# Two tail units of a bilinear interaction kernel moved within the hand-written order

## The chip, the core and the metric

The kernel runs on one core of a Trainium2 chip. The metric is device time in microseconds (us) of one launch, from the first to the last instruction and what lies around them. Inputs and outputs lie in the chip's memory (HBM); the host only rearranges them.

## What is computed

For each of 512 samples, 200 feature vectors of 64 numbers are multiplied by a 64x64 matrix of their own field, and each result is scored against all 200 feature vectors of the sample. All is float32.

```python
def _L0_rec_ref(feature, weight):        # feature (512, 200, 64), weight (200, 64, 64)
    bilinear = jnp.einsum('bie,ied->bid', feature, weight)
    out = jnp.einsum('bid,bjd->bij', bilinear, feature)
    return out                           # (512, 200, 200), 82 MB
```

## The kernel before

The samples are worked through in 4 groups of 128. In a group, the 200 fields of the first factor are taken in 3 chunks of 64 fields, and a tail of 8 fields (192 to 199). There are four kinds of units of TensorE work, and each writes one pair of PSUM banks (a unit number n uses the pair n mod 4):

- a **mix** unit (L263 to L288) multiplies 16 fields by their weights, 64 matmul rows in the profile (two for each float32 matmul in the program). Four mix units make the `mixed` operand of one chunk. ScalarE and VectorE copy each into `mixed` (L367 to L378).
- a **score** unit (L311 to L326), 16 matmul rows, scores four samples of a chunk. Two of them make an output tile: its first half is copied from PSUM to SBUF by ScalarE, its second by VectorE (L357 to L360). A chunk has 8 output tiles. Tile 1.4 is here the tile with t = 4 (the fifth) of chunk 1.
- a **tail_mix** unit (L298 to L309) does the 8 fields of the tail, once in a group, and the copies go into `tails`.
- two **tail** units per group (L328 to L344), 64 matmul rows each, score the tail fields of all samples of the group. They make one output tile together, the first unit's half copied by ScalarE and the second's by VectorE (L362 to L365).

A function `walk` (L74 to L96) is the order of all units, written by hand. TensorE, ScalarE and VectorE all run it, so a unit stands at the same place in each queue. While chunk c is scored, the mix units of the next chunk are put in behind tiles 1, 3, 5 and 6, and tail_mix behind tile 6 of chunk 0. `TAIL_CHUNK` and `TAIL_AFTER` (L42, L43) say behind which tiles the two tail units stand.

An output tile is 0.8 MB. It is written to one of 6 slots in SBUF, and the slot is the number of the tile mod 6. A tile gets its number (the list OUT_TILES, L114 and L119) when its *second* unit comes in the order. The copy of either half waits until the tile with the number six lower has been stored from that slot and has landed (L353, L354). SyncE issues the stores in the order of the numbers, when both halves are copied (L190 to L200), two issues of 400 KB each. Behind the stores of the tiles of chunk 0 it issues the next group's first loads, and behind those of chunk 2 (L206 to L210) the next group's second loads. In chunk 1 there are no loads. Group 3 has no next group, and no loads. A unit of TensorE waits for the copies of the unit four before it, which had the same banks (`wait_bank`, L233 to L240).

Of the kernel before, what the change touches and what calls it, by code (L numbers as in the profile page):

```python
# [6 lines left out]
GROUPS = 4  # L7
# [5 lines left out]
CHUNK, CHUNKS = 64, 3  # L13
# [25 lines left out]
LAST_WAITED = MIX_AFTER[(PART - CHUNK) // MIX_FIELDS]  # L39


TAIL_CHUNK = [1] * (GROUPS - 1) + [CHUNKS - 1]  # L42
TAIL_AFTER = [(2, 4)] * (GROUPS - 1) + [(5, 7)]  # L43
SLOTS = 6

WARM_UPS = 8
# [23 lines left out]
def next_chunk(g, c):  # L70
    return (g, c + 1) if c + 1 < CHUNKS else (g + 1, 0)


def walk(score, tail, mix, tail_mix):  # L74


    n = 0
    for m in range(MIX_UNITS):
        mix(n, 0, 0, m)
        n += 1  # L80
    for g in range(GROUPS):
        for c in range(CHUNKS):
            for t in range(TILES):
                for u in range(2):
                    score(n, g, c, t, u)
                    n += 1
                if c == TAIL_CHUNK[g] and t in TAIL_AFTER[g]:
                    tail(n, g, TAIL_AFTER[g].index(t))
                    n += 1
                to, chunk = next_chunk(g, c)  # L90
                if t in MIX_AFTER and to < GROUPS:
                    mix(n, to, chunk, MIX_AFTER.index(t))
                    n += 1
                if c == 0 and t == TAIL_MIX_AFTER:
                    tail_mix(n, g)
                    n += 1  # L96


def count_copies():

    copies, readers, number, tiles = [], [], {}, []

    def add(n, act, dve, banks, *key):
        a, d = copies[-1] if copies else (0, 0)
        copies.append((a + act, d + dve))
        readers.append(banks)
        number[key] = n

    def score(n, g, c, t, u):
        add(n, u == 0, u == 1, ((u,), (u,)), "score", g, c, t, u)
        if u == 1:
            tiles.append(("score", g, c, t))  # L114

    def tail(n, g, e):
        add(n, e == 0, e == 1, ((e,), (e,)), "tail", g, e)
        if e == 1:
            tiles.append(("tail", g))  # L119

    def mix(n, g, c, m):
        add(n, 1 if m % 2 == 0 else 2, 2 if m % 2 == 0 else 1, ((m % 2,), (1 - m % 2,)), "mix", g, c, m)

    def tail_mix(n, g):
        add(n, 1, 1, ((0, 1), ()), "tail_mix", g)

    walk(score, tail, mix, tail_mix)
    return copies, readers, number, tiles
# [6 lines left out]
def build(nc, x, weight, out, out_tail):  # L135
# [36 lines left out]
    with nc.Block() as block:  # L172
# [59 lines left out]
        def _(pe):  # L232
# [112 lines left out]

            warm_up()
            walk(score, tail, mix, tail_mix)

        def copies(eng, copy, engine):
# [37 lines left out]
            for n in range(MIX_UNITS):  # L387
                own = slice(n * OWN_FIELDS, (n + 1) * OWN_FIELDS)
                eng.wait_ge(w_loaded[n], 16)
                copy(w_sb[half_rows(engine), 1, own, :], w_sb[half_rows(1 - engine), 0, own, :]).then_inc(  # L390
                    w_crossed[engine], 1)
            walk(score, tail, mix, tail_mix)

        @block.scalar
# [42 lines left out]
```

## Time and profile before

| | |
|---|---|
| median of three runs | 311.1 us (307.51 to 311.19) |
| the profiled execution | 306.8 us, of which the span of instructions is 305.0 us |
| TensorE matmul busy | 243.2 us, 80% |
| VectorE busy | 152.8 us, 50% |
| ScalarE busy | 130.1 us, 43% |
| GpSimd busy | 12.5 us, 4% |
| DMA | 112.35 MB, mean 368 GB/s; the main queue's packets take 92.6% of 16 engines' span |
| mean granted TensorE clock | 0.961 of full speed |

In the profile PE is TensorE, PEld its weight loads, ACT ScalarE, DVE VectorE, POOL GpSimd and SP SyncE; "q" behind a name is its sequencer, which issues DMA. A row of the page that groups instructions has the line of the kernel, the engine, the operation, out<-in, and the count.

### The profile page before, as it was taken

How to read it: one execution, taken by the hardware profiler on the slowest of the kernel's cores; microseconds unless marked ns; L12 is line 12 of the kernel's file. 1: busy time of each engine (PE TensorE's matmuls, PEld its weight loads, DVE VectorE, ACT ScalarE, POOL GpSimd, SP SyncE). 2: the span in 40 equal slices, each digit the busy share in tenths (PEclk: the TensorE clock that was granted, in tenths of full speed). 3: DMA queues.
4: the chain of work that ended last, by engine and by line, in shares of the span. 5: the costliest groups of instructions: out<-in, count | busy, mean ns of one | idle time of the engine just before them, and what ended most of it. 6: DMA issues, size and time to landing. Idle time of an engine off the chain costs nothing.

```text
span 305.0 us, 14640 instructions
## 1 busy us (share of the span) xinstructions
PE 243.2 (80%) x6800; PEld 210.9 (69%) x6800; DVE 152.8 (50%) x180; ACT 130.1 (43%) x181; POOL 12.5 (4%) x23
## 2 busy tenths in 40 slices
PE   6839849999877586999867785898985774998990
PEld 2437749888776476878866675866885674996970
DVE  0153634556755443537644454634765554775621
ACT  2153515445544324245444243542653451665420
POOL 2004800000000000000000000000000000000000
PEclk9996997999999979899999799999999999999997
DMA  7999997999999999968999999986999999599995
GB/s 219 415 417 357 363 410 302 324 376 373 369 360 416 407 419 420 409 280 354 374 366 408 383 411 417 388 355 248 389 371 391 408 387 417 210 402 381 409 408 218
DMA packets 22172, 112.35 MB, mean 368 GB/s; under 512 B 4320, under 2 KB 4320, under 8 KB 21856
## 3 DMA queue, kind: packets, MB, share of 16 engines
q1 hardware_dynamic: 22112, 111.43, 92.6%
q8 instruction: 53, 0.87, 1.1%
q14 instruction: 7, 0.06, 0.0%
HBM read 29.49 MB, written 81.92 MB: 365 GB/s over the span
## 4 chain that ended last, share of the span: by engine, by line
PE 76%; issue 16%; DMA 2%; SPq 2%; DVE 1%; ACT 1%
PE psum L322 50%; PE psum L285 17%; PE psum L339 8%; DMA w_sb<-w_dram 2%; SPq L166 2%; PE psum L305 1%; DVE tile L355 1%; ACT mixed L376 0%; ACT w_sb L390 0%; SPq L178 0%
## 5 line engine op out<-in xcount | busy, mean ns | idle before, releaser
L322 PE MATMUL psum<-x_sb,mixed 64*64 64x200 f32 x3072 | 163.1, 351 | 14.0 <-issue 12.5
L322 PEld LDWEIGHTS psum<-x_sb,mixed 64*64 64x64 f32 x3072 | 133.3, 139 | 27.9 <-issue 17.9
L355 DVE COPY tile<-psum 128x800 f32<-128x800 f32 x100 | 99.2, 992 | 88.6 <-PE psum L322 79.8
L355 ACT COPY tile<-psum 128x800 f32<-128x800 f32 x100 | 82.4, 826 | 70.2 <-PE psum L322 54.0
L285 PE MATMUL psum<-x_sb,w_sb 64*64 64x64 f32 x3072 | 64.4, 221 | 35.1 <-issue 34.2
L285 PEld LDWEIGHTS psum<-x_sb,w_sb 64*64 64x64 f32 x3072 | 61.7, 134 | 40.5 <-issue 37.7
L376 ACT COPY mixed<-psum 64x512 f32<-64x512 f32 x48 | 27.8, 580 | 43.2 <-PE psum L285 42.6
L376 DVE COPY mixed<-psum 64x512 f32<-64x512 f32 x48 | 33.1, 689 | 16.7 <-PE psum L285 15.5
L378 ACT COPY mixed<-psum 128x512 f32<-128x512 f32 x24 | 14.1, 586 | 36.3 <-PE psum L285 36.2
L378 DVE COPY mixed<-psum 128x512 f32<-128x512 f32 x24 | 16.6, 691 | 22.3 <-PE psum L285 22.2
L339 PE MATMUL psum<-x_sb,tails 128*32 128x200 f32 x512 | 25.0, 342 | 0.1
L339 PEld LDWEIGHTS psum<-x_sb,tails 128*32 128x32 f32 x512 | 16.9, 108 | 7.5 <-issue 2.5
L296 PE MATMUL psum<-tails 128*128 128x512 f32 x16 | 9.9, 790 | 2.6 <-POOL tails L216 2.6
L227 POOL COPY w_sb<-w_sb 64x512 f32<-64x512 f32 (+1 forms) x18 | 10.5, 586 | 25.7 <-DMA w_sb<-w_dram 24.1
L296 PEld LDWEIGHTS psum<-tails 128*128 128x128 f32 x16 | 4.0, 260 | 7.6 <-issue 5.0
L390 DVE COPY w_sb<-w_sb 64x512 f32<-64x512 f32 x4 | 1.7, 422 | 13.9 <-DMA w_sb<-w_dram 13.9
L305 PE MATMUL psum<-x_sb,w_sb 64*64 64x64 f32 x128 | 5.6, 240 | 2.2 <-issue 2.2
L390 ACT COPY w_sb<-w_sb 64x512 f32<-64x512 f32 x4 | 2.5, 617 | 11.3 <-DMA w_sb<-w_dram 11.2
L305 PEld LDWEIGHTS psum<-x_sb,w_sb 64*64 64x64 f32 x128 | 5.1, 155 | 2.3 <-issue 2.3
L385 DVE COPY tails<-psum 64x512 f32<-64x512 f32 x4 | 2.8, 694 | 3.9 <-PE psum L305 3.9
L385 ACT COPY tails<-psum 64x512 f32<-64x512 f32 x4 | 2.3, 580 | 2.6 <-PE psum L305 2.6
L216 POOL MEMSET tails<- 128x2048 f32 x1 | 1.8, 1804 | 0.3 <-POOLq L418 0.3
(5 smaller groups left out, 1.7 us busy)
## 6 DMA issues: line engine op xcount, KB each, us to landing
out_dram<-tile SPq DMA_DIRECT2D x192, 400.0 KB, 5.6
x_sb<-x_dram SPq DMA_DIRECT2D x64, 400.0 KB, 6.9
out_tail_dram<-tile SPq DMA_DIRECT2D x8, 400.0 KB, 4.2
w_sb<-w_dram SPq DMA_DIRECT2D x1, 1152.0 KB, 15.2
w_sb<-w_dram SPq DMA_DIRECT2D x4, 256.0 KB, 7.3
w_sb<-w_dram SPq DMA_DIRECT2D x1, 1024.0 KB, 13.1
```

Source lines behind the costliest of these rows:

```text
L166: eng.dma_start(x_sb[strip, 2 * (g % 2), quads], x[g, 0, strip, quads]).then_inc(part0_loaded[g % 2], 16)
L227: nc.gpsimd.tensor_copy(w_sb[half_rows(h), 1, own, :], w_sb[half_rows(1 - h), 0, own, :]).then_inc(w_crossed[2], 1)
L285: last = nc.tensor.matmul(psum[half_rows(h ^ swap), bank + swap, r * HALF_SAMPLES:(r + 1) * HALF_SAMPLES], w_field(h, field), x_field(g, h ...
L296: nc.tensor.matmul(psum[:, 2 * BANK_PAIRS - 1, :], zeros[:, 0:128], zeros, start=True, stop=True)
L305: last = nc.tensor.matmul(psum[half_rows(h), n % BANK_PAIRS * 2, r * HALF_SAMPLES:(r + 1) * HALF_SAMPLES], w_field(h, TAIL_FIRST + r), x_f ...
L322: last = nc.tensor.matmul(psum[half_rows(pair), n % BANK_PAIRS * 2 + h, a * FIELDS:(a + 1) * FIELDS], mixed[half_rows(h), (CHUNKS * g + c) ...
L339: last = nc.tensor.matmul(psum[column * TAIL_TILE:(column + 1) * TAIL_TILE, n % BANK_PAIRS * 2 + half_unit, piece * FIELDS:(piece + 1) * F ...
L355: copy(tile[:, k % SLOTS, engine], psum[:, bank:bank + 2, 0:2 * FIELDS]).then_inc(copied[engine], 1)
L376: copy(to[half_rows(h)], source[half_rows(1 - h)]).then_inc(copied[engine], 1)
L378: copy(to, source).then_inc(copied[engine], 1)
L385: copy(tails[half_rows(engine), :, 0:4:3, engine, :], source).then_inc(copied[engine], 1)
L390: copy(w_sb[half_rows(engine), 1, own, :], w_sb[half_rows(1 - engine), 0, own, :]).then_inc(w_crossed[engine], 1)
```

## The change

For the groups 0 to 2, the first tail unit stands behind tile 4 of chunk 1 instead of tile 2, and the second behind tile 1 of chunk 2 instead of tile 4 of chunk 1. For that, the table names a chunk with each tile. Group 3 is as before: behind tiles 5 and 7 of chunk 2. Lines behind the table are one line higher up in the changed kernel (L355 is L354, L339 is L338).

```diff
-TAIL_CHUNK = [1] * (GROUPS - 1) + [CHUNKS - 1]
-TAIL_AFTER = [(2, 4)] * (GROUPS - 1) + [(5, 7)]
+TAIL_AFTER = [((1, 4), (2, 1))] * (GROUPS - 1) + [((2, 5), (2, 7))]
...
-                if c == TAIL_CHUNK[g] and t in TAIL_AFTER[g]:
-                    tail(n, g, TAIL_AFTER[g].index(t))
+                if (c, t) in TAIL_AFTER[g]:
+                    tail(n, g, TAIL_AFTER[g].index((c, t)))
```

On TensorE, from tail_mix of group 0 (L305) on, before; L322 is score (16 matmuls of the program for a tile), L285 mix, L339 a tail unit:

```order
L305 MATMUL psum<-x_sb,w_sb 64x64 x16
L322 MATMUL psum<-x_sb,mixed 64x200 x48
L285 MATMUL psum<-x_sb,w_sb 64x64 x32
L322 MATMUL psum<-x_sb,mixed 64x200 x16
L339 MATMUL psum<-x_sb,tails 32x200 x32
L322 MATMUL psum<-x_sb,mixed 64x200 x16
L285 MATMUL psum<-x_sb,w_sb 64x64 x32
L322 MATMUL psum<-x_sb,mixed 64x200 x16
L339 MATMUL psum<-x_sb,tails 32x200 x32
L322 MATMUL psum<-x_sb,mixed 64x200 x16
L285 MATMUL psum<-x_sb,w_sb 64x64 x32
L322 MATMUL psum<-x_sb,mixed 64x200 x16
```

The same place in the changed kernel:

```order
L304 MATMUL psum<-x_sb,w_sb 64x64 x16
L321 MATMUL psum<-x_sb,mixed 64x200 x48
L284 MATMUL psum<-x_sb,w_sb 64x64 x32
L321 MATMUL psum<-x_sb,mixed 64x200 x32
L284 MATMUL psum<-x_sb,w_sb 64x64 x32
L321 MATMUL psum<-x_sb,mixed 64x200 x16
L338 MATMUL psum<-x_sb,tails 32x200 x32
L321 MATMUL psum<-x_sb,mixed 64x200 x16
L284 MATMUL psum<-x_sb,w_sb 64x64 x32
L321 MATMUL psum<-x_sb,mixed 64x200 x16
L284 MATMUL psum<-x_sb,w_sb 64x64 x32
L321 MATMUL psum<-x_sb,mixed 64x200 x48
```

The first tail unit has moved behind two more tiles and a mix unit, to where the second was; the second has left the chunk and follows the last row shown (tile 7 of chunk 1 and tiles 0 and 1 of chunk 2 are the x48).

On ScalarE, from tile 1.2 of group 0 on, before. L355 is the copy of a tile's half, and slot_out is the semaphore of the slot that it writes; the second row is the first tail unit's:

```order
L355 COPY tile<-psum 128x800 [waits slot_out4,unit_ready]
L355 COPY tile<-psum 128x800 [waits slot_out1,unit_ready]
L355 COPY tile<-psum 128x800 [waits slot_out5,unit_ready]
L376 COPY mixed<-psum 64x32x16 [waits unit_ready]
L376 COPY mixed<-psum 64x32x16
L355 COPY tile<-psum 128x800 [waits slot_out0,unit_ready]
L355 COPY tile<-psum 128x800 [waits slot_out2,unit_ready]
```

The same place in the changed kernel, with the first tail unit's copy the second of the two that one row counts (x2):

```order
L354 COPY tile<-psum 128x800 [waits slot_out4,unit_ready]
L354 COPY tile<-psum 128x800 [waits slot_out5,unit_ready]
L375 COPY mixed<-psum 64x32x16 [waits unit_ready]
L375 COPY mixed<-psum 64x32x16
L354 COPY tile<-psum 128x800 [waits slot_out0,unit_ready] x2
L354 COPY tile<-psum 128x800 [waits slot_out1,unit_ready]
```

The tail's copy stood between the slots 4 and 5 and wrote slot 1; it now stands directly behind the copy of tile 1.4 and writes the slot of that tile, slot 0.

## Rows read from the trace of the kernel before

**Rows 1.** The page: the chain of work that ended last, by engine.

```profile
PE 76%; issue 16%; DMA 2%; SPq 2%; DVE 1%; ACT 1%
```

**Rows 2.** Busy sums by chunk, from chunk 2 of group 0 on; columns in the header.

```profile
core 0: us, PE busy (x) PEld busy (x) DVE busy (x) ACT busy (x) POOL busy (x), PEclk, DMA share, GB/s
...
72.00:91.50 19.50, 16.94 (x516) 15.20 (x512) 12.06 (x14) 10.10 (x15) 0.00 (x0) 1.00 0.98 367
91.50:120.00 28.50, 19.45 (x550) 17.27 (x547) 13.72 (x16) 11.37 (x16) 0.00 (x0) 0.94 1.02 415
120.00:143.65 23.65, 23.52 (x641) 19.46 (x640) 11.94 (x14) 10.14 (x15) 0.00 (x0) 0.93 0.87 351
143.65:165.60 21.95, 16.52 (x518) 15.48 (x514) 12.00 (x14) 10.89 (x15) 0.00 (x0) 1.00 0.99 380
165.60:191.30 25.70, 18.95 (x548) 18.25 (x549) 12.69 (x15) 10.25 (x15) 0.00 (x0) 0.93 1.02 406
191.30:216.50 25.20, 22.84 (x650) 18.20 (x642) 12.93 (x15) 10.59 (x16) 0.00 (x0) 1.00 0.84 334
216.50:236.65 20.15, 15.99 (x516) 14.91 (x513) 12.07 (x14) 10.07 (x15) 0.00 (x0) 1.00 1.00 384
```

**Rows 3.** Timeline of TensorE, chunk 1 of groups 1, 2, 0: start, us, what.

```profile
127.32 3.11 PE L339 MATMUL psum<-x_sb,tails 128*32 128x200 f32 x64
130.37 1.66 PE L322 MATMUL psum<-x_sb,mixed 64*64 64x200 f32 x32
...
139.78 1.60 PE L322 MATMUL psum<-x_sb,mixed 64*64 64x200 f32 x32
...
206.66 0.58 PE L322 MATMUL psum<-x_sb,mixed 64*64 64x200 f32 x7 [1.29 <-issue]
...
212.61 0.71 PE L322 MATMUL psum<-x_sb,mixed 64*64 64x200 f32 x12
...
67.80 0.52 PE L322 MATMUL psum<-x_sb,mixed 64*64 64x200 f32 x6
```

**Rows 4.** Timeline of SyncE, issues of stores: start, us, what.

```profile
58.92 0.94 SPq L200 DMA_DIRECT2D out_dram<-tile  x1
63.58 1.11 SPq L200 DMA_DIRECT2D out_dram<-tile  x2
66.58 1.85 SPq L200 DMA_DIRECT2D out_tail_dram<-tile  x2
135.56 1.11 SPq L200 DMA_DIRECT2D out_dram<-tile  x2
138.57 1.11 SPq L200 DMA_DIRECT2D out_tail_dram<-tile  x2
208.37 1.11 SPq L200 DMA_DIRECT2D out_dram<-tile  x2
211.40 1.11 SPq L200 DMA_DIRECT2D out_tail_dram<-tile  x2
```

**Rows 5.** DMA issues at 136.08, 208.88, 286.04, each alone; last column us to landing.

```profile
out_dram<-tile SPq DMA_DIRECT2D x1, 400.0 KB, 4.4
...
out_dram<-tile SPq DMA_DIRECT2D x1, 400.0 KB, 3.1
...
out_dram<-tile SPq DMA_DIRECT2D x1, 400.0 KB, 6.0
```

**Rows 6.** Busy sums around the places where stores run dry, columns as in rows 2.

```profile
57.00:66.00 9.00, 9.00 (x240) 7.04 (x233) 3.16 (x4) 3.64 (x5) 0.00 (x0) 1.00 1.01 415
...
131.50:134.00 2.50, 2.50 (x104) 2.23 (x100) 1.64 (x2) 1.64 (x3) 0.00 (x0) 1.00 0.30 114
...
139.50:147.00 7.50, 7.50 (x255) 6.64 (x251) 5.72 (x8) 5.05 (x7) 0.00 (x0) 1.00 0.95 380
...
190.00:204.00 14.00, 12.93 (x360) 10.95 (x356) 6.79 (x8) 6.12 (x8) 0.00 (x0) 1.00 1.01 399
```

**Rows 7.** Timeline of ScalarE: the first tail unit's copy in group 3 and two more.

```profile
292.13 2.29 ACT L355 COPY tile<-psum 128x800 f32<-128x800 f32 x3 [3.89 <-DMA out_dram<-tile]
```

## The prediction, made before the changed kernel ran

> **What bounds the kernel now.** I read the page first. The chain that ended last is 76% TensorE work and 16% "issue", pauses that no semaphore of the program explains, and almost no copy or transfer [rows 1]. That would say: TensorE is the bound, so move work into its pauses. I then cut the span at the first scoring matmul of each chunk and read the busy sums per stage [rows 2]. It shows two regimes. In chunks 0 and 2 of the groups 0 to 2 the 16 DMA engines are saturated (share 0.98 to 1.02), while TensorE stands still for 2.6 us (72.0 to 91.5), 9.05 us (91.5 to 120.0), 5.4 us (143.65 to 165.6) and 6.8 us (165.6 to 191.3). These stages also carry the loads of the next group. Chunk 1 has no loads and both tail units: there TensorE is busy nearly throughout (23.52 of 23.65 us in group 1, 22.84 of 25.20 in group 2) and the DMA engines are at 0.87 and 0.84, that is 3.1 and 4.0 us of nothing to move. So the group from 91.5 to 165.6, 74.1 us, is some 71 us of saturated DMA time and 3 us in which the stores ran dry. A DMA gap is made up for nowhere, as far as the stages on both sides stay at a share of 1; a TensorE gap is, in the pauses of chunks 0 and 2. I therefore price the change by what it does to the moments at which the DMA engines run dry and start again, and keep the TensorE view as a rival.
>
> **What the tail units cost where they stand.** One is 3.05 us of TensorE (127.32 to the next unit's start at 130.37) [rows 3]. Its copy is 0.83 us on ScalarE (in group 3: 2.29 for that one and two more in a row, 0.76 to 0.83 each; I take 0.83) [rows 7], and each store of a tile takes two issues on SyncE.
>
> **The change.** No instruction is added or removed; two are moved, in three groups.
>
> *Second unit, to chunk 2.* 3.05 us of TensorE and 0.8 MB of store leave chunk 1 and come in between tiles 1 and 2 of chunk 2. DMA time is conserved. TensorE there idles 2.6, 5.4 and (216.5 to 236.65) 4.2 us [rows 2], so the unit can go under DMA time already spent; cost 0 in the DMA view. If that cover is gone it is 3.05 us per group, 9.2 in all. The next group's second load is one issue that follows on SyncE behind tile 1 of chunk 2 and ahead of the tail's store, so it isn't delayed. VectorE's copy there finds its slot free, since ScalarE has waited for the same slot in chunk 1.
>
> *First unit, behind tile 4 of chunk 1.* This is the one with a price. Output tiles are numbered when they are complete, and slot = number mod 6. Before, tiles 1.0 to 1.4 completed ahead of the tail, so the first unit's copy behind tile 1.2 wrote the slot of tile 0.7, stored three tiles earlier. Now five tiles complete between the first unit and the second: 1.5, 1.6, 1.7, 2.0, 2.1. The tail's number is that of tile 1.4 plus 6, the order on ScalarE shows it (two copies in a row wait for slot_out0). So ScalarE's copy must wait for the landing of a store whose second half VectorE has not even copied yet. Queued behind it on ScalarE: its half of tile 1.5, without which SyncE cannot store 1.5, nor anything behind it. TensorE goes on for tail unit, tile 1.5 and mix unit 2 (four banks' depth), then its first unit of tile 1.6 waits for the tail's copy.
>
> How long from the first issue of a store to its landing? The trace has it at three loads. Lightly loaded, group 2: issue 208.37, second half issued 208.88, landed 3.1 later, together 3.6 us. After a gap that had just closed, group 1: 135.56, 136.08 plus 4.4, together 4.9 us. Saturated, in group 3, whose first tail unit waits in the same way, but for a tile with three more behind it (2.2, with 2.3 to 2.5 between): the second half issued at 286.04 plus 6.0, and the first 0.9 us earlier (as long as the saturated issue at 58.92 took, 0.94), together 6.9 us; ScalarE stood 3.89 us for it until 292.13 [rows 4, 5, 7]. That row proves the mechanism; the new place has no tile in between at all.
>
> Then, from landing L: tail copy 0.83 and the copy of 1.5 at 0.83, with 0.05 us steps: the store of 1.5 is issued at L + 1.75, and TensorE begins tile 1.6 at L + 0.9. I compare with the tail's store before (which was the first to restart the DMA engines there) and with tile 1.6's start.
>
> Group 0. DMA share is 1.01 from 57 to 66 [rows 6]: there is a backlog, and the same bytes lie ahead of tile 1.4, so they can't be done before 66. Tile 1.4's store started at 63.58; 3.05 earlier is 60.5, but SyncE ends the issue of tile 1.2 only at 59.86 (58.92 + 0.94), and a pair of such issues takes 1.9 us and some gap, so 1.3 at 59.9, 1.4 at 61.9 [rows 4]. I take the saturated 6.9: L = 68.8, next store 70.55 against 66.58: **+4.0 us**. Tile 1.6: 69.7 against 67.80.
> Group 1. 135.56 - 3.05 = 132.5. The engines ran dry from 131.5 on (share 0.30 to 134) [rows 6], and now would be filled earlier: between 4.9 and 6.9, I take 5.9. L = 138.4, next store 140.15 against 138.57: **+1.6**. Tile 1.6: 139.3 against 139.78.
> Group 2. 208.37 - 3.05 = 205.3, less the pause of 1.29 us in tile 1.4 [rows 3], which comes once in 128 matmul rows or so and moves behind the tail unit, where the new wait hides it: 204.0. The engines were full until then (1.01 from 190 to 204). 5.9 again: L = 209.9, next store 211.65 against 211.40: **+0.25**. Tile 1.6: 210.8 against 212.61.
>
> Sum 5.85. Against it: after their restart the engines still had small gaps in 139.5 to 147 (0.05 of 7.5 us = 0.4) which the later, denser stores close; for three groups I take 0.9, a little less than three times that since group 0 has a backlog. Net **+5 us**. The profiled execution is 306.8 us (span 305.0 and 1.8 around it): 311.8. The median is 311.1 of runs from 307.51 to 311.19, so the profiled one is at the low end; 5 us on the median is **316.1 us**, 1.6% up.
>
> Bounds of this case: with the shortest row (3.6) in groups 1 and 2, L is 136.1 and 207.6, and in group 0 not before 66, where the bytes are done; the shifts are +1.2, -0.7 and -2.0, less 0.9: -2.4. With 6.9 everywhere: 4.0 + 2.6 + 1.25 = +7.9, with no credit. So 308.7 to 319.
>
> **A rule against it.** The rows make a landing 3.6 to 6.9 us from the first issue. The Trainium skill (DMA: Bandwidth & Descriptors, "Anatomy of one DMA — SWDGE (gpsimd) path") fits one transfer as 2.0 us plus bytes over 436 GB/s, which by my estimate is 3.9 us for the two halves of a tile back to back. The trace agrees only where the engines were nearly idle (3.6); at a share of 1 it is 6.9. By that rule the wait all but disappears, which is rival 3.
>
> **Rivals.**
> 1. *TensorE carries the time, the pauses take up the second unit.* For: the chain. Against: DMA share 1 where it pauses. The starts of tile 1.6 give +1.9, -0.5, -1.8: -0.4 in all, 310.7.
> 2. *TensorE carries, and the pauses of chunk 2 stay as they are.* They come about once in 128 matmul rows whatever the rows do, so 64 more make no room: -0.4 + 9.2 = +8.8, 319.9. For: they are called "issue" and have nothing to do with a semaphore. Against: they are short or absent in chunk 1, where the DMA engines have room.
> 3. *Faster: the landing is quick and TensorE carries.* With 3.6 us in groups 1 and 2 and 4.9 from 60.5 in group 0, tile 1.6 starts at 66.3, 137.0 and 208.5: -1.5, -2.8, -4.1, sum -8.4, 302.7. It decides when the wait ends before TensorE comes to tile 1.6, 3.05 us earlier than now; L must be under 63.9, 135.8 and 207.4. For: chunk 1 of group 1 is busy on TensorE for all its length. Against: the backlog at 57 to 66 and before 204.
>
> **Chances.** Forecast case 0.46, rival 1 0.20, rival 2 0.20, rival 3 0.12, others 0.02. Two per cent (about what a measurement of this kernel can tell from no change) is 6.2 us: 304.9 and 317.3. Below lies most of rival 3: 0.11. Above lie a good third of the forecast case and most of rival 2: 0.34. Within: 0.55. The range leaves out rival 3 and the far end of rival 2: 307 to 321.
>
> **What would show it.** A new row "ACT tile <- DMA out_dram", three times more, 4 to 6 us each behind tile 1.4; TensorE standing ahead of tile 1.6 some 5, 2.6 and 2.5 us (69.7, 139.3 and 210.8 less the starts that TensorE could reach, 64.75, 136.7 and 208.3); chunk 1's DMA share lower than now or the same though the chunk has one tail unit less; chunk 2 at a share of 1. Wrong if chunk 1 is 3 us shorter in all three groups with no such wait (rival 3), or if chunk 2 grows by 3 us with its DMA share under 0.95 (rival 2).

## The result and the profile after

The changed kernel takes 321.24 us (median of 4 runs, 316.86 to 323.75) against 310.57 us (307.51 to 311.19): ratio 1.032, interval 1.020 to 1.045, so some 10 us slower. Most kernels here have some executions that are slower by one to three per cent, and the ratios in this text compare only the fast ones, so a ratio can differ a little from that of two medians. (The 310.57 us is the median of the three runs known at the forecast and a fourth.) The profiled execution has 319.98 us and a span of 318.2 us, 13.2 us over the one before, at the high end of the difference.

The timeline of ScalarE in the changed kernel, every wait that the landing of a store ended (start us, us, what, in brackets the idle time ahead of it):

```profile
67.83 1.55 ACT L354 COPY tile<-psum 128x800 f32<-128x800 f32 x2 [7.32 <-DMA out_dram<-tile]
142.84 1.55 ACT L354 COPY tile<-psum 128x800 f32<-128x800 f32 x2 [7.40 <-DMA out_dram<-tile]
219.67 1.55 ACT L354 COPY tile<-psum 128x800 f32<-128x800 f32 x2 [6.48 <-DMA out_dram<-tile]
305.91 2.29 ACT L354 COPY tile<-psum 128x800 f32<-128x800 f32 x3 [4.71 <-DMA out_dram<-tile]
```

Before, only the last of them was there, in group 3 [rows 7]. Each of the three new ones is a first tail unit's copy, and the copy of tile 1.5 that had stood behind it follows at once (x2). The timeline of TensorE has what waits for it, tile 1.6 in groups 0, 1 and 2:

```profile
68.71 1.68 PE L321 MATMUL psum<-x_sb,mixed 64*64 64x200 f32 x32 [1.62 <-ACT tile L354]
...
143.72 1.92 PE L321 MATMUL psum<-x_sb,mixed 64*64 64x200 f32 x32 [2.62 <-ACT tile L354]
...
220.55 1.67 PE L321 MATMUL psum<-x_sb,mixed 64*64 64x200 f32 x32 [1.44 <-ACT tile L354]
```

Before, these starts had no idle time ahead [rows 3]. The chain of work now has transfers in it:

```profile
PE 67%; issue 15%; DMA 9%; SPq 3%; DVE 2%; ACT 2%; ACTq 0%
```

against 76% TensorE and 2% DMA [rows 1]. The issues of the stores of tile 1.4 and of the next tile in groups 0, 1, 2, from the timeline of SyncE:

```profile
61.34 1.90 SPq L199 DMA_DIRECT2D out_dram<-tile  x2
69.41 1.11 SPq L199 DMA_DIRECT2D out_dram<-tile  x2
136.39 1.12 SPq L199 DMA_DIRECT2D out_dram<-tile  x2
144.42 1.11 SPq L199 DMA_DIRECT2D out_dram<-tile  x2
213.67 1.78 SPq L199 DMA_DIRECT2D out_dram<-tile  x2
221.25 1.11 SPq L199 DMA_DIRECT2D out_dram<-tile  x2
```

From the end of the one issue to the start of the next SyncE issues nothing for 6.2, 6.9 and 5.8 us in the middle of each chunk 1; behind tile 1.4 it was 1.9 us before (66.58 less 64.69) [rows 4]. And the busy sums by chunk, with the columns of rows 2; chunks 1 and 2 of groups 0, 1 and 2:

```profile
49.55:72.65 23.10, 19.70 (x585) 16.76 (x577) 12.00 (x14) 9.93 (x16) 0.00 (x0) 1.00 0.76 295
72.65:97.10 24.45, 20.71 (x580) 18.63 (x580) 13.04 (x15) 10.88 (x15) 0.00 (x0) 0.93 0.98 376
...
121.95:149.15 27.20, 20.98 (x577) 17.73 (x580) 11.02 (x13) 10.28 (x15) 0.00 (x0) 0.94 0.79 318
149.15:173.15 24.00, 19.32 (x579) 16.68 (x573) 12.97 (x15) 10.45 (x15) 0.00 (x0) 0.98 0.94 357
...
200.95:224.50 23.55, 20.46 (x586) 17.62 (x578) 12.03 (x14) 9.86 (x15) 0.00 (x0) 0.96 0.77 295
224.50:250.00 25.50, 20.30 (x580) 18.36 (x580) 13.06 (x15) 10.87 (x15) 0.00 (x0) 0.95 1.00 384
```

Two things stand in them. Chunk 1 has a tail unit less and is still no shorter in sum (73.85 us for three; before it was 71.05, with the 22.2 us of group 0 in the row below), and its DMA share fell to 0.76 to 0.79. Chunk 2 grew in all three groups, 24.45, 24.0 and 25.5 us against 19.5, 21.95 and 20.15 [rows 2], far more in groups 0 and 2 than the 3 us of the unit that came in. The row of the kernel before for chunk 1 of group 0:

```profile
49.80:72.00 22.20, 22.16 (x646) 18.84 (x637) 13.06 (x15) 10.52 (x16) 0.00 (x0) 1.00 0.84 325
```

### The profile page after: what moved, and what is told of

It reads as the page before. It is cut to its first block, busy times and chain, and to the rows that moved or that the text cites. A ratio compares the mean times of both kernels' runs of the same rounds, so it can differ in the third digit from the quotient of the medians.

```text
span 318.2 us, 14640 instructions
## 1 busy us (share of the span) xinstructions
PE 251.6 (79%) x6800; PEld 218.6 (69%) x6800; DVE 152.9 (48%) x180; ACT 129.2 (41%) x181; POOL 12.5 (4%) x23
## 4 chain that ended last, share of the span: by engine, by line
PE 67%; issue 15%; DMA 9%; SPq 3%; DVE 2%; ACT 2%; ACTq 0%
PE psum L321 46%; PE psum L284 15%; DMA out_dram<-tile 7%; PE psum L338 4%; DMA w_sb<-w_dram 2%; SPq L165 2%; DVE tile L354 2%; ACT tile L354 1%; PE psum L304 1%; SPq L199 1%; ACT mixed L375 1%; DVE mixed L375 0%; DVE mixed L377 0%; ACT w_sb L389 0%; SPq L177 0%
## 5 line engine op out<-in xcount | busy, mean ns | idle before, releaser
L321 PE MATMUL psum<-x_sb,mixed 64*64 64x200 f32 x3072 | 169.7, 362 | 20.9 <-issue 9.9
L321 PEld LDWEIGHTS psum<-x_sb,mixed 64*64 64x64 f32 x3072 | 140.3, 144 | 34.9 <-issue 14.8
L354 DVE COPY tile<-psum 128x800 f32<-128x800 f32 x100 | 99.2, 992 | 104.8 <-PE psum L321 96.0
L354 ACT COPY tile<-psum 128x800 f32<-128x800 f32 x100 | 82.2, 827 | 78.7 <-PE psum L321 50.0
L284 PE MATMUL psum<-x_sb,w_sb 64*64 64x64 f32 x3072 | 65.7, 223 | 30.5 <-issue 29.4
L377 ACT COPY mixed<-psum 128x512 f32<-128x512 f32 x24 | 14.1, 588 | 37.4 <-PE psum L284 37.4
L338 PE MATMUL psum<-x_sb,tails 128*32 128x200 f32 x512 | 25.6, 343 | 1.8 <-issue 1.8
L338 PEld LDWEIGHTS psum<-x_sb,tails 128*32 128x32 f32 x512 | 17.5, 108 | 9.2 <-issue 4.6
L304 PE MATMUL psum<-x_sb,w_sb 64*64 64x64 f32 x128 | 5.3, 233 | 3.3 <-issue 3.3
L389 ACT COPY w_sb<-w_sb 64x512 f32<-64x512 f32 x4 | 2.5, 618 | 11.6 <-DMA w_sb<-w_dram 11.5
```

The costliest lines, as they stand in the source:

```text
L284: last = nc.tensor.matmul(psum[half_rows(h ^ swap), bank + swap, r * HALF_SAMPLES:(r + 1) * HALF_SAMPLES], w_field(h, field), x_field(g, h ...
L304: last = nc.tensor.matmul(psum[half_rows(h), n % BANK_PAIRS * 2, r * HALF_SAMPLES:(r + 1) * HALF_SAMPLES], w_field(h, TAIL_FIRST + r), x_f ...
L321: last = nc.tensor.matmul(psum[half_rows(pair), n % BANK_PAIRS * 2 + h, a * FIELDS:(a + 1) * FIELDS], mixed[half_rows(h), (CHUNKS * g + c) ...
L338: last = nc.tensor.matmul(psum[column * TAIL_TILE:(column + 1) * TAIL_TILE, n % BANK_PAIRS * 2 + half_unit, piece * FIELDS:(piece + 1) * F ...
L354: copy(tile[:, k % SLOTS, engine], psum[:, bank:bank + 2, 0:2 * FIELDS]).then_inc(copied[engine], 1)
L377: copy(to, source).then_inc(copied[engine], 1)
```

## The experiments

All ratios are to the kernel before, on the same chip, with 95% intervals.

**Is it the wait?** Three kernels. The first two choose the slot of a tile by age: at the tile's first half, take the slot whose tile has the lowest number, so the one stored longest ago.

```diff
+def place_tiles():
+    held, uses, slot_of, use_of = [-1] * SLOTS, [0] * SLOTS, {}, {}
...
+    def take(tile):
+        s = min(range(SLOTS), key=lambda s: held[s])
+        slot_of[tile], use_of[tile] = s, uses[s]
+        held[s], uses[s] = TILE_OF[tile], uses[s] + 1
...
-                if k >= SLOTS:
-                    eng.wait_ge(slot_out[k % SLOTS], STRIP_STORES * (k // SLOTS))
+                slot, before = SLOT_OF[name], USE_OF[name]
+                if before:
+                    eng.wait_ge(slot_out[slot], STRIP_STORES * before)
```

*The changed order with oldest slots.*

> The changed order of units, but each output tile takes the slot whose tile was stored longest ago at the moment of its first half, instead of number mod 6. The first tail unit behind tile 1.4 then waits for tile 0.7 (five tiles earlier) and not for tile 1.4 itself. Theory A (the slot wait costs it all, the second unit is hidden in chunk 2): the three ScalarE waits of 5 to 7 us are gone, and tile 1.5's store is issued some 1.5 us earlier than in the kernel before; 300 to 306 us, so faster than the kernel before by 2 to 3%. Theory B (the second unit is not hidden in chunk 2 and costs 3 us per group there): the same waits are gone, but the time is 308 to 314 us, no better than before.

Measured: 0.998 (0.993 to 1.003). Its trace has not one ScalarE wait for a store any more. So the loss is gone, and nothing is won: both theories were right on the wait, and the time (median 310.05 us) is the one of theory B. Its busy sums by chunk, same columns and same chunks as above:

```profile
47.70:70.40 22.70, 20.59 (x582) 17.66 (x578) 11.96 (x14) 10.41 (x15) 0.00 (x0) 0.98 0.89 354
70.40:95.35 24.95, 20.39 (x583) 18.35 (x577) 13.04 (x15) 10.61 (x15) 0.00 (x0) 0.95 0.94 360
...
120.65:143.95 23.30, 19.22 (x576) 16.51 (x575) 11.06 (x13) 10.10 (x15) 0.00 (x0) 1.00 0.92 372
143.95:166.80 22.85, 19.43 (x579) 17.12 (x577) 12.98 (x15) 10.92 (x15) 0.00 (x0) 1.00 0.97 362
...
193.05:216.05 23.00, 19.47 (x584) 16.85 (x575) 11.97 (x14) 10.59 (x16) 0.00 (x0) 1.00 0.88 358
216.05:239.65 23.60, 19.55 (x584) 16.52 (x580) 13.07 (x15) 10.14 (x15) 0.00 (x0) 1.00 0.99 380
```

In chunk 2 TensorE's idle time is 4.56, 3.42 and 4.05 us, 12.0 in sum, against 2.56, 5.43 and 4.16, 12.15, before [rows 2]: the pauses did not take the unit up, they stand beside it, and the three stages are 9.8 us longer. In chunk 1, where 9.2 us of TensorE work left, 7.2 us of idle time came in (9.7 us now, 59.3 busy of 69.0, for 2.5 before in the same three stages). Nearly all of it is "issue", pauses for which the profile shows no releaser. The DMA share there rose to about 0.9. The work left the chunk, and pauses came in where it had been.

*The order of the kernel before with oldest slots*, the control.

> The order of units of the kernel before, with the same choice of slots by oldest store: the control for the other one. Only the wait of 3.9 us in group 3 has reason to shrink (the copy then waits for tile 2.0 instead of 2.2). Both theories: 307 to 311 us, within 1% of before. If it is faster by 2% or more, the choice of slots gains something that has nothing to do with the moved units.

Measured: 0.9995 (0.993 to 1.006). The choice of slots alone is worth nothing, so the first kernel's ratio is the order's.

*The wait put back.* The changed order with oldest slots, and one wait added by hand:

```diff
+                    if e == 0 and g < GROUPS - 1:
+                        last = "score", g, 1, 4
+                        eng.wait_ge(slot_out[SLOT_OF[last]], STRIP_STORES * (USE_OF[last] + 1))
```

> The changed order with oldest slots (ratio 0.998), and one wait added by hand: ScalarE's copy of the first tail unit waits until tile 1.4's store has landed, as in the change. Units, slots of the other tiles and transfers are those of the fast variant. If the wait is the whole cause: ratio 1.025 to 1.035, as the change (1.032). If the slot assignment itself (which tile follows which in a slot) mattered, it stays at 0.995 to 1.01.

Measured: 1.040 (1.030 to 1.051), above the 1.025 to 1.035 that I had forecast, with an interval that overlaps that of the change. Every other slot, unit and transfer is as in the kernel with 0.998, so the wait is enough for the whole of the loss. The waits are a little longer than in the change, 8.68, 7.70 and 6.99 us. For two of the three the profile names "issue" and not the transfer; in group 0 the second half of tile 1.4's store, issued at 60.98, landed 6.9 us later, at 67.88, and the copy began at 67.95 (in group 2, 212.44 plus 5.9 is 218.34, and the copy began at 218.44):

```profile
67.95 1.55 ACT L373 COPY tile<-psum 128x800 f32<-128x800 f32 x2 [8.68 <-issue]
...
143.21 1.55 ACT L373 COPY tile<-psum 128x800 f32<-128x800 f32 x2 [7.70 <-DMA out_dram<-tile]
...
218.44 1.55 ACT L373 COPY tile<-psum 128x800 f32<-128x800 f32 x2 [6.99 <-issue]
```

**How much per microsecond of wait?** Slots by number mod 6 again, so that the place of the second unit sets which tile's landing the first one waits for.

*Second unit behind tile 1.7; the first waits for tile 1.2.*

```diff
-TAIL_AFTER = [((1, 4), (2, 1))] * (GROUPS - 1) + [((2, 5), (2, 7))]
+TAIL_AFTER = [((1, 4), (1, 7))] * (GROUPS - 1) + [((2, 5), (2, 7))]
```

> Slots by number mod 6 as in the changed kernel, but the second tail unit behind tile 1.7: the first unit's copy then waits for the landing of tile 1.2 (two tiles and a mix unit earlier) instead of tile 1.4. Theory A: landing of tile 1.2 is 5 to 6 us earlier than that of 1.4, so the ScalarE wait in chunk 1 shrinks from 5 to 7 us to 0 to 1 us and the time is that of the same order with oldest slots within 1%, 306 to 311 us. If the wait itself is not the cause, it stays at 317 to 321 us.

Measured: 1.009 (1.004 to 1.0135), within 1% of the same order with oldest slots (below), as theory A has it. But the wait did not shrink to 0 to 1 us everywhere: there are two outside group 3, of 4.99 us in group 1 and of 4.70 us in group 2.

```profile
136.70 1.55 ACT L354 COPY tile<-psum 128x800 f32<-128x800 f32 x2 [4.99 <-PE psum L321]
...
208.80 1.55 ACT L354 COPY tile<-psum 128x800 f32<-128x800 f32 x2 [4.70 <-DMA out_dram<-tile]
```

The profile puts the first down to TensorE (L321, a score unit). The tail unit that this copy reads was done at about 134.5, though (TensorE began the next unit at 134.46), and the second half of tile 1.2's store, issued at 128.96, has this row:

```profile
out_dram<-tile SPq DMA_DIRECT2D x1, 400.0 KB, 7.7
```

It landed at 136.66, and the copy began at 136.70. So this is a wait for the store too. In group 0 the copy waited only for its tail unit (2.42 us).

*The same order with oldest slots*, so without a wait.

> Oldest slot again; first tail unit behind tile 1.4 as in the change, second behind tile 1.7, so still in front of chunk 2. Against the kernel with the second behind tile 2.1 it shows what two tiles' distance is worth. Theory A: TensorE's 3 us per group are on both sides of the boundary nearly the same, but the DMA engines run dry in chunk 1 for 3 to 4 us as before: 306 to 311 us, 1 to 2% slower than with the second unit in chunk 2. Theory B: equal to it within 1%.

Measured: 1.0004 (0.9935 to 1.007), equal within the noise to the 0.998 with the second unit behind tile 2.1. That is theory B's forecast: on which side of the chunk boundary the second unit stands makes no difference that can be measured here.

*Second unit behind tile 2.0; the first waits for tile 1.3.*

```diff
+TAIL_AFTER = [((1, 4), (2, 0))] * (GROUPS - 1) + [((2, 5), (2, 7))]
```

> Slots by number mod 6, first unit behind tile 1.4, second behind tile 2.0: the first unit's copy waits for the landing of tile 1.3, which is stored one tile and a mix unit (about 2.5 us) before tile 1.4. Theory A: a ScalarE wait of about 3 to 4 us where the change has 5 to 7 us and the variant with the second unit behind 1.7 had nearly none; ratio 1.015 to 1.022, between these two (1.009 and 1.032). If the wait costs only when it is longer than some cover, it falls on one of the two.

Measured: 1.016 (1.011 to 1.021), as theory A has it, with waits of 4.35, 5.12 and 4.25 us, longer than the 3 to 4 forecast:

```profile
65.25 1.56 ACT L354 COPY tile<-psum 128x800 f32<-128x800 f32 x2 [4.35 <-DMA out_dram<-tile]
139.48 1.55 ACT L354 COPY tile<-psum 128x800 f32<-128x800 f32 x2 [5.12 <-DMA out_dram<-tile]
212.89 1.55 ACT L354 COPY tile<-psum 128x800 f32<-128x800 f32 x2 [4.25 <-DMA out_dram<-tile]
```

*The change in group 1 alone.*

```diff
+TAIL_AFTER = [((1, 2), (1, 4)), ((1, 4), (2, 1)), ((1, 2), (1, 4))] + [((2, 5), (2, 7))]
```

> The change in group 1 alone; the groups 0 and 2 keep the order of the kernel before, slots by number mod 6. Theory A (each wait costs its own DMA gap, carried to the end): a third of the loss of the whole change, ratio 1.011 to the kernel before (1.005 to 1.016), one extra ScalarE wait of 5 to 7 us. If the waits only add up when they follow each other (for instance by leaving TensorE's clock low more and more often), one alone costs under 0.5%.

Measured: 1.011 (0.9997 to 1.0225), with one such wait of 6.55 us, ahead of the copy at 142.25. The value is one third of the whole, but the interval reaches down to no loss at all, so this run alone does not decide between the two readings.

A part of such a wait costs nothing, because ScalarE would stand idle there anyway until the tail unit is computed. How long, the changed order with oldest slots shows at the same three copies, where nothing else is waited for:

```profile
63.15 1.74 ACT L373 COPY tile<-psum 128x800 f32<-128x800 f32 x2 [3.48 <-PE psum L356]
...
137.34 1.73 ACT L373 COPY tile<-psum 128x800 f32<-128x800 f32 x2 [2.90 <-PE psum L356]
...
209.91 1.72 ACT L373 COPY tile<-psum 128x800 f32<-128x800 f32 x2 [3.19 <-PE psum L356]
```

Put together, with the idle time of ScalarE ahead of these copies where a store was waited for (profiled execution, groups 0 to 2), what is left of it without the 3.48, 2.90 and 3.19 us, and the loss as (ratio - 1) of the kernel before on that chip, with its interval:

| kernel | first unit waits for | ScalarE wait, us | beyond the usual idle, us | ratio | loss, us |
|---|---|---|---|---|---|
| oldest slots | nothing late | 0 | 0 | 0.998 | -0.6 (-2.2 to 0.9) |
| second unit at 1.7 | tile 1.2 | 9.7 | 3.6 | 1.009 | 2.7 (1.3 to 4.2) |
| group 1 alone | tile 1.4 | 6.6 | 3.7 | 1.011 | 3.4 (-0.1 to 6.9) |
| second unit at 2.0 | tile 1.3 | 13.7 | 4.2 | 1.016 | 5.0 (3.5 to 6.6) |
| the change | tile 1.4 | 21.2 | 11.6 | 1.032 | 10.0 (6.1 to 13.9) |
| wait put back | tile 1.4 | 23.4 | 13.8 | 1.040 | 12.5 (9.2 to 15.7) |

Of the whole wait, 0.3 to 0.5 us of each microsecond reaches the end. Of what goes beyond the usual idle it is 0.75 to 1.2, about all of it. The intervals are wide, and each wait is that of one execution, so the second number is a fit and not a law, but one rule fits all five kernels: the first 3 us are free, and the rest is paid in full.

**What carries the time outside the wait?** The prediction rests on the DMA engines as the bound. Five kernels ask that.

*No second loads*: the loads of half of the inputs are left out for the groups 1 to 3.

```diff
-                    if c == CHUNKS - 1:
-                        for n in range(X_LOADS):
-                            if PART1_AFTER[n] == t:
-                                load_part1(sp, g + 1, n)
...
-                pe.wait_ge(part1_loaded[p], 16 * X_STRIPS * (g + 1))
+                pe.wait_ge(part1_loaded[p], 16 * X_STRIPS)
```

> The kernel before without the loads of the second half of the inputs for the groups 1 to 3 (24 issues, 9.8 MB of 112 MB; the groups use group 0's data there). TensorE's and the copies' work is unchanged. It asks what chunks 2 and 0 are bound by. If by the bytes (the DMA engines' share of 1): 9.8 MB at 415 GB/s is 23.7 us, so 285 to 292 us. If by TensorE and pauses of its own in instruction supply: 300 us or more.

Measured: 0.945 (0.9375 to 0.9525), 292.1 us. That is 16 to 17 us of 23.7, at the slow edge of the forecast for the bytes; the forecast for TensorE alone is out. TensorE's work is unchanged; what shrank is its pauses in mix and score units, from 34.2 and 12.5 us to 24.4 and 7.6. The list of waits, here (L279 is mix, L316 score; us in sum, times, longest):

```profile
PE psum L279 <- issue: 24.4, 18, 3.6
...
PE psum L316 <- issue: 7.6, 10, 1.2
```

The list of waits of the kernel before:

```profile
PE psum L285 <- issue: 34.2, 21, 3.6
...
PE psum L322 <- issue: 12.5, 8, 2.8
```

The two sums are 46.7 and 32.0 us. How far such a sum moves by itself: with all transfers left in, it is 38.2 us in the order with the second unit at 1.7 and oldest slots, whose time is that of the kernel before, and 52.3 in the kernel with three loads moved, below. So 32.0 lies outside the scatter, but how much of the 14.7 us the loads are worth is uncertain.

*No second tail unit*: two of its 32 matmuls are left in the groups 0 to 2.

```diff
-                    for piece in range(2):
-                        for pair in range(2):
-                            for column in range(4):
+                    cut = e == 1 and g < GROUPS - 1
+                    for piece in range(1 if cut else 2):
+                        for pair in range(1 if cut else 2):
+                            for column in range(1 if cut else 4):
...
-                                    x_sb[:, g % 2:g % 2 + 2, quad, :, pair], start=pair == 0, stop=pair == 1)
+                                    x_sb[:, g % 2:g % 2 + 2, quad, :, pair], start=pair == 0, stop=cut or pair == 1)
```

> The kernel before, with 2 of the 32 matmuls of the second tail unit left in the groups 0 to 2 (its output half is stored, but not computed); copies, stores and waits are unchanged. It takes 8.6 us of TensorE work out of the busy chunks 1 and no byte of output. If TensorE carries the time there (rival 2's reading: moving the unit only moves its cost): 8 to 9 us less, ratio 0.970 to 0.975. If the DMA engines carry it: the stores come 3 us earlier, run into the same transfers later, and the ratio is 0.985 to 1.0.

Measured: 0.985 (0.9735 to 0.996), 4.7 us of the 8.6. The interval reaches into both forecasts, from 1.2 to 8.2 us, so this kernel does not tell them apart; its middle is half of the work taken out. The profiled execution has TensorE busy for 243.2 us, as before, with 180 matmul rows fewer, at a mean granted clock of 0.938 instead of 0.961.

*Three of the first loads moved into the DMA gap of chunk 1.*

```diff
+PART0_AFTER = ((0, 0), (0, 1), (0, 2), (0, 3), (0, 4), (1, 3), (1, 4), (1, 5))
...
-                    if c == 0:
-                        load_part0(sp, g + 1, t)
+                    for n in range(X_LOADS):
+                        if PART0_AFTER[n] == (c, t):
+                            load_part0(sp, g + 1, n)
```

> The kernel before, with three of the eight first loads of the next group moved from behind tiles 0.5, 0.6 and 0.7 to behind tiles 1.3, 1.4 and 1.5, where the DMA engines run dry. No other edit. If the DMA gaps of chunk 1 (3 to 4 us in each group) are what the kernel loses, three loads fill 3 us of it in each of three groups: 300 to 304 us, ratio 0.97 to 0.985. If DMA time is not the bound, no change (0.995 to 1.005).

Measured: 1.019 (1.008 to 1.029). Slower, where I had forecast 2% faster. The gap that I had taken for the loss is no smaller for the bytes put into it: chunk 1 of groups 0 and 1 is at a DMA share of 0.77 and 0.81 (0.84 and 0.87 before), and only group 2 rose, to 0.92 from 0.84:

```profile
49.60:73.70 24.10, 22.64 (x648) 18.57 (x640) 13.03 (x15) 10.59 (x16) 0.00 (x0) 1.00 0.77 293
124.65:149.85 25.20, 22.48 (x642) 18.69 (x641) 11.95 (x14) 10.93 (x15) 0.00 (x0) 1.00 0.81 300
197.70:223.60 25.90, 23.05 (x647) 18.84 (x638) 13.02 (x15) 10.59 (x16) 0.00 (x0) 1.00 0.92 358
```

All three are longer than before, 24.1, 25.2 and 25.9 us against 22.2, 23.65 and 25.2. Chunk 0 of the groups 1 and 2, with 1.2 MB less to move, is not shorter in sum, 27.85 and 26.8 us against 28.5 and 25.7 [rows 2]. TensorE's pauses in mix and score units are 52.3 us (37.4 and 14.9) where they were 46.7, and its matmuls are busy for 248.0 us instead of 243.2. What made the pauses longer I did not settle.

*Fewer bytes in the queues*, with d = 2 or 3:

```diff
+                if k >= d:
+                    sp.wait_ge(slot_out[(k - d) % SLOTS], STRIP_STORES * ((k - d) // SLOTS + 1))
```

> The kernel before, but SyncE issues the store of tile k only when that of tile k-2 has landed, so that at most two tiles (1.6 MB) and a load are in the queues. Theory C (TensorE's pauses, one in about 128 matmul rows, are its instruction blocks of 16 KB coming late behind the stores): the pauses shrink from 46.7 us in sum to under 30, but the DMA engines idle more, since a landing takes 4 to 7 us for 2 us of data: time 305 to 325 us. Theory D (the pauses have nothing to do with the queue): their sum stays within 10% of 46.7 us.

> As before, with three tiles in the queues (2.4 MB, 6 us of data at 400 GB/s), which covers a landing of 5 to 6 us. Theory C: pauses shrink a little and the DMA engines are hardly starved: 300 to 309 us. Theory D: pauses as before, 308 to 312 us.

Measured: 1.048 (1.034 to 1.063) with two tiles, 0.996 (0.990 to 1.003) with three. With two, the pauses of mix and score units fell from 46.7 to 21.8 us, as theory C has it, but the copy engines now wait 58 us for stores (48.2 on ScalarE, 10.0 on VectorE; before it was 3.9):

```profile
ACT tile L356 <- DMA out_dram<-tile: 48.2, 15, 9.1
...
PE psum L286 <- issue: 19.7, 14, 3.8
...
PE psum L323 <- issue: 2.1, 3, 1.0
```

It isn't a clean proof, since a pause that falls into such a wait is no longer seen. With three tiles the pauses are 43.2 us and the time 308.15 us, which both theories allow. No kernel here that computes the whole result beats the one before by more than its interval.

## Why the prediction was right, and what it got wrong

**The wait: right.** Its place, its cause and what queues behind it are as forecast. With oldest slots the loss is gone (0.998), and with the wait put back it is there again (1.040), so the wait is shown to be the whole of it.

**How long a landing takes: right.** From the first issue of tile 1.4's store: group 0, 62.06 plus 5.7 is 67.76, so 6.4 us from 61.34 (I took 6.9); group 1, 6.4 (136.91 plus 5.9; I took 5.9); group 2, 5.9 (214.18 plus 5.4; I took 5.9). These are the second halves' issues, each alone, with us to landing last:

```profile
out_dram<-tile SPq DMA_DIRECT2D x1, 400.0 KB, 5.7
...
out_dram<-tile SPq DMA_DIRECT2D x1, 400.0 KB, 5.9
...
out_dram<-tile SPq DMA_DIRECT2D x1, 400.0 KB, 5.4
```

The 3.6 us of the lightly loaded row, and the 3.9, by my estimate, that the fit of the Trainium skill gives (DMA: Bandwidth & Descriptors, "Anatomy of one DMA — SWDGE (gpsimd) path"), did not come back in any group. Rival 3 is out.

**The signs it named.** The three new rows are there, but with 7.32, 7.40 and 6.48 us and not "4 to 6". That figure did not follow from the prediction's own landings (68.8, 138.4, 209.9): counted from the end of ScalarE's copy of tile 1.4, 3.05 us earlier than before (63.10, 135.09 and 206.23), they make 6.4 to 8.8 us. TensorE stood ahead of tile 1.6 for 1.6, 2.6 and 1.4 us, where it had 5, 2.6 and 2.5. Chunk 1's DMA share fell, as it said. Chunk 2 was at 0.98, 0.94 and 1.00. The sign against it, 3 us more in chunk 2 at a share under 0.95, did not tell the two views apart: chunk 2 grew by 4.95 and 5.35 us at 0.98 and 1.00, and by 2.05 at 0.94.

**The size: half of it.** The forecast was +5 us; the runs give +10 (6 to 14). The likeliest class was "within 2%", at 0.55, and the measured 3.2% lies above it. The range went up to 321 us: the ratio of 1.032 on 310.57 us is 320.6, just inside, and the median of the four runs, 321.24, just outside. So it was the wide range that held it, drawn to take in most of rival 2, and not the sum. The terms of the sum, in the profiled execution: the next store against the same store before is +2.8, +5.85 and +9.85 us. Less the shift that the chunk already began with (-0.25, +1.95 and +9.65) this is 3.1, 3.9 and 0.2, in sum 7.2, where I had 4.0, 1.6 and 0.25, in sum 5.85. The sum at the restarts came out near, in part by luck, since group 0 was 0.9 us too high and group 1 2.3 too low. Three things failed:

- In group 1, that everything up to tile 1.4 comes 3.05 us earlier. Its store came only 1.1 us earlier (136.39 less 1.95 is 134.44, against 135.56), since TensorE now paused on the way (rows below), where it had not before.
- "DMA time is conserved ... cost 0 in the DMA view" for the second unit. Chunk 2 grew by 12.35 us in sum (TensorE busy 10.9 more, idle 1.5 more), and in the kernel without the wait by 9.8 us with TensorE's idle time unchanged at 12 us. The unit was not hidden; that is rival 2's mechanism. Without the wait the rest of the kernel gives it back in part (chunk 1 is 2.05 us shorter in sum and chunk 0 of the groups 1 and 2 2.65 us) and the ratio is 0.998. With the wait chunk 1 is 2.8 us longer instead, and the cost in chunk 2 stays.
- The credit of 0.9 us for denser stores after the restart. Behind the restart of group 0 the shift did fall by 0.9 us (2.8 to 1.95, up to chunk 1 of group 1). Behind the restarts in groups 1 and 2 it grew, by 3.8 us (5.85 to 9.65, up to the start of chunk 1 of group 2) and 3.5 us (9.85 to 13.35, up to the end of chunk 2). So the credit of 0.9 is a cost of 6.4, and with the 7.2 at the restarts and the -0.25 of the start this makes the 13.35.

The two pauses of the first point, from the timeline of TensorE in the changed kernel:

```profile
127.95 3.09 PE L321 MATMUL psum<-x_sb,mixed 64*64 64x200 f32 x64 [1.98 <-DVE mixed L375]
...
133.60 1.66 PE L321 MATMUL psum<-x_sb,mixed 64*64 64x200 f32 x32 [1.61 <-DVE mixed L377]
```

The VectorE copies that the profile names had ended 0.4 and 0.9 us before. The two pauses stand 128 matmul rows apart, and 128 rows behind another of 1.70 us at 121.93, so I take them for the pauses of the last section.

The claim behind all three, "A DMA gap is made up for nowhere ... a TensorE gap is", does not hold as it stands: 23.7 us of transfers taken out gave 16 to 17, 8.6 us of TensorE gave about 5 (1.2 to 8.2), and moving bytes from a full stage to one with room gave a loss. What the wait alone costs in the profile is best read against the same order without it: from the start of chunk 1 of group 0 to the end of chunk 2 of group 2 it is 200.45 us against 191.95, 8.5 more, of which 4.85 lie in the chunks 1, 2.55 in the chunks 2 and 1.1 in the chunks 0 between them.

**The rivals.** Rival 1 (-0.4 us) is out. Rival 2, +8.8 us at a chance of 0.20, was nearest in size, and its rule, that a unit costs the same in chunk 2 as in chunk 1, also gives the 0.998 of the kernel without the wait (3.05 us out, 3.05 in). What I held against it, that the pauses are short or absent in chunk 1 because the DMA engines have room there, failed: chunk 1 of group 1 now has two, of 1.98 and 1.61 us, at a DMA share of 0.79. Its premise, that TensorE carries the time, is not shown: TensorE's work taken out gave 1.2 to 8.2 of 8.6 us, and transfers taken out gave the most of theirs. It deserved more than 0.20.

**TensorE's clock.** The mean granted clock is 0.937 in the changed kernel's profile and 0.961 before, and the matmuls are busy for 251.6 us against 243.2, so one could put 8.4 of the 13.2 us down to the clock. The kernel with the wait put back speaks against it as the cause: it has a span of 317.8 us at a clock of 0.955 with 244.3 us of matmuls. There the same time shows as idle.

## What to carry to other kernels

When a buffer's slot is chosen by the number of a finished item, but the item is begun earlier, moving the begin and the end apart turns "six tiles ago" into "just now". List, for every first write, which transfer it waits for; the order of waits shows it (two copies in a row on one slot) before anything runs. A wait of an engine that looks 43% busy can reach the end, because what is queued behind it feeds both the next store and the next matmul; here about 3 us of each were free, since the engine would have been idle, and the rest was paid. And the releaser that a profile names for a wait is worth a check where the named engine had been done for long: one of the store waits here stood under TensorE's name. Last, a stage with idle time on one engine is no free place for its work until it is known what makes the idle time.

## What the runs showed of the hardware

TensorE's pauses go by count: not every block of 128 matmul rows has one, but where they occur in a row they are that far apart. In the kernel before, chunk 2 of group 1, the timeline of TensorE has them at 148.69, 153.79 and 159.16, and between two of them lie 128 matmul rows (the rows from 148.69 to 151.60 count 1, 3, 1, 61 and 62):

```profile
148.69 0.27 PE L285 MATMUL psum<-x_sb,w_sb 64*64 64x64 f32 x1 [0.99 <-issue]
148.69 0.42 PE L322 MATMUL psum<-x_sb,mixed 64*64 64x200 f32 x3
148.80 0.22 PE L285 MATMUL psum<-x_sb,w_sb 64*64 64x64 f32 x1
148.86 3.01 PE L322 MATMUL psum<-x_sb,mixed 64*64 64x200 f32 x61
151.60 1.14 PE L285 MATMUL psum<-x_sb,w_sb 64*64 64x64 f32 x62
153.79 0.27 PE L285 MATMUL psum<-x_sb,w_sb 64*64 64x64 f32 x1 [1.04 <-issue]
```

With the weight loads these are 256 instructions. The page of the profile counts 6800 matmul rows and as many weight loads, which is 53.1 times 256, and 53 packets with 0.87 MB, 16.4 KB each, on the queue q8 named "instruction". A transfer of 16 KB (0.02 MB in the row) on this queue falls between 146.2 and 147.3, none between 148 and 151, and the next between 151.2 and 152.5, each some 1.3 to 2.6 us ahead of the end of a pause. In the changed kernel they fall between 125 and 126 and between 131 and 132, ahead of the ends at 127.95 and 133.60. The Trainium skill (Runtime: NRT & Kernel Launch, "Instruction fetch mechanics") says that instructions come in blocks of 16 KB, 256 of them, and that the cost is mostly hidden. The block size agrees with these rows; "mostly hidden" does not hold here, where "issue" is 16% of the chain [rows 1] and the pauses in mix and score units shrink when there is less to load (46.7 us to 32.0 without the second loads). That the blocks come late because they stand behind the stores fits this, but it was not tried in isolation and stays open.
